# Re-ordering the start-up of an attention and mixture-of-experts kernel: query projections, heads and fills

## What is computed

```
q = heads(layernorm(x) @ Wq.T + bq)            # 16 heads of 16
k, v = heads(ctx @ Wk.T + bk), heads(ctx @ Wv.T + bv)
p = softmax(where(mask == 0, -1e9, q k^T / sqrt(16)))
x = x + (p v) @ Wo.T + bo                      # one batch after the other
f = layernorm(x)
w, e = top2(softmax(f @ router_w))             # 8 experts
x = x + sum over the two: w * (silu(f @ w1[e]) @ w2[e])
```

## Time and profile before

| | us |
|---|---|
| runs | 520.27, 520.72, 523.5 |
| median | 520.72 |
| the profiled execution's own time | 524.17 |
| its span (first to last instruction) | 522.4 |

### The profile page before, as it was taken

The page is one execution under the profiler, slowest core; times in us unless marked ns, Lnnn a source line. Parts: engine busy times, 40 slices in busy tenths (PEclk is TensorE's granted clock), DMA queues, the critical chain, the costliest instruction groups (busy, mean ns, idle before and its releaser), DMA issues.

```text
span 522.4 us, 10734 instructions
## 1 busy us (share of the span) xinstructions
PE 435.2 (83%) x4179; PEld 390.2 (75%) x4179; DVE 355.2 (68%) x756; ACT 256.0 (49%) x323; POOL 211.2 (40%) x170
## 2 busy tenths in 40 slices
PE   2567669999999999999999975477999999999700
PEld 2355458888888888888877874477999999999600
DVE  2776555777787777777776576944777777777425
ACT  3240244655665665656555533015566666666200
POOL 7270460223233333332100070052588887886410
PEclk9795787999999999999999988558999999999965
DMA  7849473777888887677430043072677777775148
GB/s 181 239 138 286 137 194 82 157 165 166 182 168 173 174 180 170 159 167 145 110 83 22 4 156 127 0 261 82 212 242 243 246 240 251 247 248 189 63 156 286
DMA packets 75026, 87.89 MB, mean 168 GB/s; under 512 B 20144, under 2 KB 66896, under 8 KB 74976
## 3 DMA queue, kind: packets, MB, share of 16 engines
q1 hardware_dynamic: 69040, 74.36, 54.8%
q0 software_dynamic: 4032, 11.02, 5.8%
q10 hardware_dynamic: 1904, 1.84, 1.0%
HBM read 51.58 MB, written 16.90 MB: 131 GB/s over the span
## 4 chain that ended last, share of the span: by engine, by line
PE 72%; DVE 11%; issue 7%; DMA 4%; POOL 2%; SPq 1%; ACT 1%; POOLq 0%; DVEq 0%; ACTq 0%
PE ps L1336 32%; PE ps L1396 11%; PE ps L1425 8%; PE ps L1411 8%; PE ps L1359 7%; DMA chosen_y<-y_rows 2%; PE ps L1644 2%; DVE neg_max L931 1%; SPq L527 1%; PE ps L1438 1%; PE ps L1627 1%; DVE x_rows_sb L978 1%; DVE w_lo L1232 1%; DMA keep<-keep_scratch 1%; PE ps L1446 1%
## 5 line engine op out<-in xcount | busy, mean ns | idle before, releaser
L931 DVE TENSOR_REDUCE neg_max<-ps 112x1 f32<-112x376 f32 x256 | 132.6, 546 | 45.0 <-PE ps L1396 41.2
L734 ACT ACTIVATE probs<-ps 125x1344 f32<-125x1344 f32 x64 | 82.8, 1293 | 57.6 <-PE ps L1411 56.7
L1396 PE MATMUL ps<-k_stack,q_stack 98*112 98x376 f32 x256 | 85.4, 376 | 11.0 <-issue 6.4
L555 POOL TENSOR_TENSOR k_lo<-k_f,k_hi 128x752 fp32r<-128x752 f32 x16 | 28.8, 1800 | 136.6 <-ACT k_hi L708 134.1
L679 POOL DMA_INDIRECT y_rows<-y_out,y_row_of_row x42 | 66.1, 1575 | 32.9 <-DVE y_out L1247 21.6
L1396 PEld LDWEIGHTS ps<-k_stack,q_stack 98*112 98x112 f32 x256 | 43.0, 181 | 25.1 <-DVE neg_max L931 14.3
L671 POOL DMA_INDIRECT rows<-xn_rows,token_of_row x42 | 42.1, 1003 | 48.5 <-DVE y_row_of_row L1191 32.2
L1411 PE MATMUL ps<-q_stack,k_stack 100*125 100x224 f32 x384 | 54.4, 278 | 1.2 <-ACT probs L734 0.9
L1336 PE MATMUL ps<-w_hi,h_hi 128*128 128x256 f32 x168 | 49.6, 295 | 5.6 <-issue 3.7
L1411 PEld LDWEIGHTS ps<-q_stack,k_stack 100*125 100x125 f32 x384 | 50.3, 191 | 2.3 <-ACT probs L734 1.7
L1336 PE MATMUL ps<-flat_t_hi,w_hi 128*128 128x256 f32 x168 | 48.9, 291 | 2.8 <-DVE flat_t_lo L1227 2.8
(11 more groups left out here) (191 smaller groups left out, 1005.9 us busy)
## 6 DMA issues: line engine op xcount, KB each, us to landing
w_raw<-w SPq DMA_DIRECT2D x42, 512.0 KB
k_stack<-k_hi SPq DMA_DIRECT2D x64, 188.0 KB, 4.7
k_stack<-k_lo SPq DMA_DIRECT2D x32, 188.0 KB, 5.5
ctx_raw<-ctx_t SPq DMA_DIRECT2D x32, 187.5 KB, 2.6
q_stack<-q_scratch SPq DMA_DIRECT2D x32, 168.0 KB
q_scratch<-q_hi SPq DMA_DIRECT2D x16, 224.0 KB, 3.1
xn_rows<-xn SPq DMA_DIRECT2D x14, 256.0 KB, 2.5
chosen_y<-y_rows SPq DMA_DIRECT2D x14, 256.0 KB, 5.4
```

Of the source, the lines that this page charges most:

```text
L555: pool.tensor_tensor(kl[:, :, :], kf[:, :, :], kh[:, :, :].bitcast(F32), ALU.subtract)\
L734: act.activation(pf[j % 2][:, :, :], ps[0:CT, BK_ST:BK_ST + KT, 0:4 * S], ACT.Exp).then_inc(pf_ready, 1)
L931: dve.tensor_reduce(neg_max[:, s:s + 1], ps[0:S, BK_MAX + s % 2, 0:CP], AX.X, ALU.max, negate=True).then_inc(max_read, 1)
L1396: pe.matmul(ps[0:S, BK_MAX + a, 0:CP], qs[b.ring][0:R_MAX, q, S * a:S * (a + 1)], ks[b.ring][0:R_MAX, q, :], start=True, stop=True).then_i ...
```

## The change

- The queries' weights are scaled by 1/4 as they are split (ACT `activation` with scale, DVE with multiply and subtract), and the bias once, so that a query leaves PSUM finished: ACT writes the high part straight from PSUM with the bias, and DVE the low part from PSUM, the bias and the high part. `q_f`, `queries` and POOL's `query_low` are gone. Both now work half by half, as do `x_high` and `x_low`.
- The rows of group 0 are normalised by DVE as before, those of groups 1 to 3 by ACT (x*rstd + nbias, four instructions; DVE makes the small `nbias`).
- Batch 0's `q_stack` is filled straight from `q_hi` and `q_lo` in SBUF (`stack_first_queries`, six transfers), not through the scratch; only from batch 1 on the scratch is read.
- `x` comes in as four loads, `keep` is made and written first, the queries' weights come before the biases, and the mask rows later. The output's weights and the router's move from the ramp's end into turn 1 on ACT and DVE.
- The low part of the first context goes from POOL to DVE, and POOL makes six fills at once after the mask rows. ACT takes a square root of a constant first, which loads its table there.
- PE has the heads of batch 0 in pairs among the query groups 1 to 3; the last half of group 3 comes after head 15 and `max_transpose`. SP writes `stack_max` of batch 0 before group 3's writes.

The core of the diff:

```diff
             def x_high(g):
-                act.wait_ge(xt_done, g + 1)
-                act.copy(xh[g % 2][:, :, :], ps[:, 0:2, 0:SG]).then_inc(xh_ready, 1)
+                for k in range(KD):
+                    act.wait_ge(xt_done, KD * g + k + 1)
...
+                    act.copy(xh[g % 2][:, k, :], ps[:, k, 0:SG]).then_inc(xh_ready, 1)
...
-                act.copy(qh[g % 2][:, :, :], qf[:, :, :]).then_inc(qh_ready, 1)
+                act.activation(qh[g % 2][:, t, :], ps[:, (2, BK_OUT)[t], 0:SG], ACT.Identity, bias=bq_c[:, t:t + 1])\
+                    .then_inc(qh_ready, 1)
...
+            def normalise_x(g):
+                act.wait_ge(nbias_ready, g)
+                for b in range(GB * g, GB * (g + 1)):
+                    last = act.activation(xr[:, b, :], xr[:, b, :], ACT.Identity, bias=nbias[0:S, b:b + 1],
+                                          scale=rstd[0:S, b:b + 1])
+                last.then_inc(xn_ready[g], 1)
...
+            def q_low(g):
 
                 for t in range(KD):
-                    dve.wait_ge(qproj_done, 2 * g + t + 1)
-                    if g and t == 0:
-                        dve.wait_ge(ql_ready, g)
-                    dve.tensor_scalar(qf[:, t, :], ps[:, (2, BK_OUT)[t], 0:SG], bq_c[:, t:t + 1], DK ** -0.5,
-                                      ALU.add, ALU.mult).then_inc(qf_ready, 1)
+                    dve.wait_ge(qh_ready, KD * g + t + 1)
+                    dve.scalar_tensor_tensor(out=ql[g % 2][:, t, :], in0=ps[:, (2, BK_OUT)[t], 0:SG],
+                                             scalar=bq_c[:, t:t + 1], in1=qh[g % 2][:, t, :].bitcast(F32),
+                                             op0=ALU.add, op1=ALU.subtract).then_inc(ql_ready, 1)
...
+            def stack_first_queries():
+
+                for a in range(KD):
+                    sp.wait_ge(qh_ready, a + 1)
+                    for c, src in enumerate((qh[0], qh[0], ql[0])):
+                        if c == 2:
+                            sp.wait_ge(ql_ready, a + 1)
+                        part = (0, 2, 1)[c]
+                        sp.dma_start(qs[0][2 * part + a:R_MASK:2 * PARTS, :, S * a:S * (a + 1)].bitcast(F32),
+                                     src[:, a, 0:S].bitcast(F32)).then_inc(q_stacked[0], 16)
...
             mask_rows()
-            ctx_low(first)
+            fill(range(0, 6))
+            key_low(first)
             pool.wait_ge(cl_ready, 1)
-            fill(range(0, 2))
-            key_low(first)
             ctx_low(second)
-            query_low(0)
-            pool.wait_ge(ql_ready, 1)
-            fill(range(2, 6))
             key_low(second)
-            query_low(1)
-            query_low(2)
             ctx_low(first.after(2))
-            query_low(3)
             for p in range(2):
                 pool.wait_ge(q_written[p], 96 * NG // 2)
...
+            ctx_low_first()
             x_stats(0)
-            normalise_x(0)
+            x_rstd(0)
+            normalise_first()
...
-            queries(0)
+            q_low(0)
             attn_weight_low(2)
+            x_stats(2)
             x_low(1)
-            x_stats(2)
-            normalise_x(2)
+            x_rstd(2)
             keys(second, 0)
             keys(second, 1)
-            queries(1)
+            maxima(first, range(0, 4))
+            q_low(1)
+            maxima(first, range(4, 6))
             x_low(2)
-            maxima(first, range(0, 8))
             x_stats(3)
-            normalise_x(3)
-            queries(2)
+            x_rstd(3)
+            maxima(first, range(6, 10))
+            q_low(2)
+            maxima(first, range(10, 14))
             x_low(3)
-            queries(3)
-            maxima(first, range(8, H))
+            maxima(first, range(14, H))
             max_rows(first)
+            q_low(3)
```

SP, at the start:

```diff
             sp.wait_ge(zeros_set, 1)
             load_ctx(first)
-            load_rows(slice(0, GB), xr_first_in)
+            load_rows(slice(0, GB), xr_in[0])
+            load_weight(1, wq_t)
+            sp.wait_ge(keep_ready, 1)
+            sp.dma_start(keep_scratch, keep_all[:, :]).then_inc(keep_written, 16)
...
+            sp.wait_ge(keep_written, 16)
+            load_keep(first)
+            load_rows(slice(GB, 2 * GB), xr_in[1])
...
-            load_rows(slice(GB, B), xr_rest_in)
-            sp.wait_ge(mask_written, 32)
-            load_keep(first)
```

More of the change, by code:

```diff
@@ L186, in xattn_moe_kernel @@
         x2 = sb("x2", [P, NT, D])
-        assert cursor["at"] <= queries_end, "x2 lies where the queries were"
+        queries_end = max(queries_end, cursor["at"])
         cursor["at"] = raw_at
@@ L438, in write_queries @@
                                      src[g % 2][:, t, :].bitcast(F32)).then_inc(q_written[g % 2], 16)
-            second = first.after(1)
+            second, third = first.after(1), first.after(2)
             sp.dma_start(m_all[:, 0:C], mask).then_inc(mask_in, 16)
@@ L779, in _, with late_weights @@
             key_high(second)
-            q_high(1)
+            normalise_x(2)
+            queries_high(1)
             x_high(2)
             x_std(3)
-            q_high(2)
+            normalise_x(3)
+            queries_high(2)
+            ctx_high(third)
             x_high(3)
-            ctx_high(first.after(2))
-            q_high(3)
-            key_high(first.after(2))
-            attn_weight(3)
-            act.wait_ge(rw_in, 16)
-            act.copy(rwh[:, :, :], rw_raw[:, :, :]).then_inc(rw_ready, 1)
+            queries_high(3)
+            key_high(third)
+            def late_weights():
+                attn_weight(3)
+                act.wait_ge(rw_in, 16)
+                act.copy(rwh[:, :, :], rw_raw[:, :, :]).then_inc(rw_ready, 1)
             def turn(b):
@@ new lines, in normalise_first @@
+            def normalise_first():
+                for b in range(GB):
+                    last = dve.tensor_scalar(xr[:, b, :], xr[:, b, :], moments[0:S, b, 0:1], rstd[0:S, b:b + 1],
+                                             ALU.subtract, ALU.mult)
+                last.then_inc(xn_ready[0], 1)
+            def x_low(g):
+                for k in range(KD):
+                    dve.wait_ge(xh_ready, KD * g + k + 1)
+                    dve.tensor_tensor(xl[g % 2][:, k, :], ps[:, k, 0:SG], xh[g % 2][:, k, :].bitcast(F32),
+                                      ALU.subtract).then_inc(xl_ready, 1)
@@ L1518, in x_transpose, with project_queries, keys @@
                                             ident[0:S, 0:S])
-                last.then_inc(xt_done, 1)
-            def project_queries(g):
-                pe.wait_ge(wl_ready, 2)
-                pe.wait_ge(xl_ready, g + 1)
-                for t in range(KD):
-                    if g >= 1:
-                        pe.wait_ge(qf_ready, 2 * g - 1 + t)
-                    m = slice(t * P, (t + 1) * P)
-                    product(ps[:, (2, BK_OUT)[t], 0:SG],
-                            [(w[:, 1, k, m], x[g % 2][:, k, :]) for k in range(KD)
-                             for w, x in ((wh, xh), (wl, xh), (wh, xl))]).then_inc(qproj_done, 1)
+                    last.then_inc(xt_done, 1)
+            def project_queries(g, t):
+                if g == 0 and t == 0:
+                    pe.wait_ge(wl_ready, 2)
+                if g:
+                    pe.wait_ge(ql_ready, KD * (g - 1) + t + 1)
+                m = slice(t * P, (t + 1) * P)
+                terms = [(w, x, k) for k in range(KD) for w, x in ((wh, xh), (wl, xh), (wh, xl))]
+                for n, (w, x, k) in enumerate(terms):
+                    if x is xl or n % 3 == 0:
+                        pe.wait_ge((xh_ready, xl_ready)[x is xl], KD * g + k + 1)
+                    last = pe.matmul(ps[:, (2, BK_OUT)[t], 0:SG], w[:, 1, k, m], x[g % 2][:, k, :],
+                                     start=n == 0, stop=n == len(terms) - 1)
+                last.then_inc(qproj_done, 1)
+            def keys(b):
+                for t in range(KD):
+                    for k in range(KD):
+                        project_keys(b, t, k)
+            second, third = first.after(1), first.after(2)
             pe.wait_ge(wl_ready, 1)
-            for t in range(KD):
-                for k in range(KD):
-                    project_keys(first, t, k)
+            keys(first)
             x_transpose(0)
-            project_queries(0)
+            project_queries(0, 0)
+            project_queries(0, 1)
             x_transpose(1)
@@ L1541, in _ @@
                 project_values(first, k3)
-            for t in range(KD):
-                for k in range(KD):
-                    project_keys(first.after(1), t, k)
-            project_queries(1)
-            x_transpose(2)
-            pe.wait_ge(filled, 6)
-            head_scores(first, range(0, 8))
-            project_queries(2)
+            keys(second)
+            pe.wait_ge(filled, 6)
+            head_scores(first, range(0, 2))
+            project_queries(1, 0)
```

(21 more changed lines are left out.)

160 lines of the change are left out of this document (94 added, 66 removed).

## The result

| | before | after |
|---|---|---|
| median, 20 runs each | 520.24 us | 517.73 us |
| ratio, 95% interval | | 0.995 (0.9928 to 0.9972) |
| profiled execution, span | 524.17, 522.4 | 518.43, 516.6 |

The change gains half a per cent, 2.6 us by the ratio (1.5 to 3.7), where 5.7 us were forecast. The time itself, 517.7 us where 515.0 was forecast, is inside the stated range, but the gain is less than half of the forecast's. One slow run of the kernel before, 710.42 us, is left out of the ratio.

A forecast was written before the change was run, and what follows sets the result against it. The chain from the last q_lo through POOL's ctx_lo to PE's restart was taken as the bound. The ramp's -6.05 us and +0.3 in turn 1 gave -5.75, so 520.72 - 5.7 = 515.0 us, range 512.5 to 517.5.

The forecast's parts named there:

- What bounds the kernel: Ramp into turn 0: PE restarts 14.85 us after the last q_lo, released by POOL's ctx_lo of batch 3.
- First part: Ramp until the first head: starts at 32.2 us (30.2 or 34.1 by the clock) instead of 41.57, gain 9.4.
- rival 3: Ramp: values' w_lo held by POOL's ctx_lo, 1.3 us lost, last group late behind heads; 522.9 us, chance 0.10.
- second meeting: Ramp: the first context's low part on DVE held beside POOL's mask rows, costing up to 1.2 us.
- Second part: Ramp from first head to last q_lo: 21.5 us at high clock, 27.3 at low, 24.4 taken.
- The ramp's sum: Last q_lo at 57.5 us instead of 63.55, PE's restart at 72.4: gain 6.05 us.
- What moves into turn 1: Output's and router's weight splitting behind turn 1: 0 if slack swallows it, 0.9 if not, 0.3 us taken.
- The forecast's own range: Whole kernel's time: 512.5 to 517.5 us, by a third of the way to either clock.
- 1: Ramp rival: fills do no harm, clock stays high, SP becomes the bound; gain 9.4, 511.3 us, chance 0.20.
- 2: Ramp rival: low clock all along, last q_lo at 62.3, gain 1.25; 519.8 us, chance 0.25 together with 4.
- 4: Turn 0 rival: the gate moves but PE is late, gain less than 6 us; chance included in 2's 0.25.
- Turns of equal length afterwards: Sign that the forecast is right: after the ramp, the attention turns all last equally long.

The follow-up runs named there:

- e11: The changed kernel run again unchanged: 517.60 us, ratio 0.9948 to the kernel before.
- e8: Changed kernel, late weights back in the ramp, POOL's k_lo and ctx_lo ahead of the last group's wait, SP stacking keys before queries in turn 0: 512.91 us.
- e4: Changed kernel with four of POOL's six early fills put behind the first group's normalisation: 516.69 us, ratio 0.9919 to the kernel before.
- e7: Changed kernel, late weights back in the ramp, POOL's ctx_lo of batch 1 waiting for the values' w_lo: 512.34 us.
- e1: Changed kernel with the output's and router's weights split at the ramp's end again, not after turn 1: 514.00 us, ratio 0.9889 to the kernel before.
- e6: Changed kernel, late weights back in the ramp, second half of query group 3 ahead of heads 14 and 15 and the transposed maxima: 512.71 us.
- e12: Same kernel as e1, run again beside e11: 515.56 us, ratio 0.9895 to the kernel before.
- e15: The kernel before, unchanged, run once more for another profile of its ramp: 520.31 us.
- e5: Changed kernel with DVE's share of the late weights after turn 2, ACT's left after turn 1: 515.02 us, ratio 0.9925 to the kernel before.

## Why the prediction was wrong

**What bounds the kernel**: right. From the last `q_lo` to PE's restart 14.85 us was forecast, 14.26 measured (14.3 to 14.5 in the eight other profiles of the new start that keep this gate). POOL's `ctx_lo` ended just ahead of the restart each time.

**First part**: too short. The first head was to come at 32.2 (30.2 or 34.1 by the clock). It came at 35.94 in the profile, at 33.38 in e11, and at 33.5 to 34.2 in six others with the same start; only e8 had 35.9 again. The terms: the normalisation ended at 16.06, the forecast's limit, not at 15.0. `keep`, which was to be there by 12, was hidden behind that; if e4's wait ahead of `k_f` is for it, it came only at 14.9. ACT's four rows took 2.07 us, not 1.44, so the copy from PSUM was no measure for this `activation`. `q_hi`'s half took 0.62, not 0.54. And the values' `w_lo` took 1.91 us, not 0.69, and ended at 27.23 instead of 25.2. From there to the first head the forecast had 5.0 us at the high clock and 8.9 at the low one, and this held: 5.15 in e7, 8.7 in the shown profile and e8, between them elsewhere.

The long `w_lo` was rival 3's mechanism, and it is real (e7). The Trainium skill, page "SBUF — State Buffer", section "Who interferes with whom", states it: a DVE instruction with two SBUF inputs contends with a GpSimd instruction that reads SBUF. Three instructions of e7 and e8 agree. It made the instruction 1.2 us longer, about the 1.3 that rival 3 gave it. But rival 3's second meeting did not come (DVE's first `ctx_lo` took 0.94 us in every profile of the new start), and its second part at the low clock, 28.2 us, did not either.

**Second part**: 24.4 us forecast, 22.9 in the profile, in e1 and in e11. In most profiles it was too long by about as much as the first was too short, so that the last `q_lo` (57.5 forecast) ended at 56.3 to 57.1; in the shown one it ended at 58.86. That the two errors met so well is luck. That the last half group pays for standing behind the heads holds (e6, 1.6 us).

**The ramp's sum**: 6.05 us forecast. The restart moved by 5.3 us in the two profiles. With the late weights back in the ramp the gain is 4.9 us by the medians (520.1 less 515.2), and 5.8 and 5.5 by the ratios of e1 and e12, so 6.05 is not excluded. What the steps left out is that the end moves with the last `q_lo` only if the clock behind the gate is the same. The changed kernel stands there for 7.5 to 8 us (5.0 in e1 and e12, where the late weights hold DVE for 2.1 us ahead of it), and in all six profiles it has the low clock after it. The old one stood 3 us with the low clock after it in three profiles of four, but not in e15. From the restart to turn 0's transposed maxima it took 8.1 to 9.3 us in those nine profiles and 6.46 in e15. How often each happens is not measured.

**What moves into turn 1: the step that failed.** It was priced at 0.3 us, at most 0.9, as work that DVE's and ACT's slack swallows. It costs 2.5 us by undoing it and 3.7 by doing it alone. The work is worth what was said, 0.3 us (e5). Left out was the wait that the move makes: what DVE's `w_lo` waits for, what is queued behind it, and that PE has no more than two banks of slack. Where the clock falls behind the stop of 1.2 us, as in two profiles of five, it doubles the loss.

**The forecast's own range** was 512.5 to 517.5, "by a third of the way to either clock". A third of the 4.9 us to either clock is 1.6, so it should have been 513.4 to 516.6; 2.5 is half of the way. The first head at the low clock adds up to 34.0, not 34.1. Neither slip changes the failed step.

**Rivals.** Neither 1 nor 2 happened as told: the fills did harm and the clock changed between its levels. Nor did 4: POOL's `ctx_lo` let PE go on. "Turns of equal length afterwards" was named as the sign of being right, and a loss beyond turn 1 as what would make the forecast wrong; this it was.

## What to carry to other kernels

Work that is moved out of a stretch where everyone waits into one where an engine is full must be priced by its waits, not only by its length. Put each engine's share behind a point where its input is long ready, and look at what is queued behind it. When a gate is opened, look for the next thing that hangs on the same event, and move that with it; alone, such an edit may show only a part of its worth. And before a gain is read from a pair of profiles, see how far each lies from its own median.

## What the runs showed of the hardware

- A stop of 1.20 us in a PE that was full is followed by the half clock in two of the five profiles that have it (the shown one and e11), and the turn then costs 3.0 us more than the others instead of 1.5.
- The same start gave a first head at 33.4 to 34.2 us in seven profiles and at 35.9 in two. The granted clock goes with it: 0.50 from 30 to 36 us in the shown one, 1.00 in e11, with PE busy for 5.45 of these 6 us in both. What sets it is open.
- POOL's memsets held four DVE `tensor_scalar` for 5.05 us (1.38 without them, in e4). DVE's `w_lo` of the queries, with two SBUF inputs, ran beside a memset in e4 at its usual 0.68, but the values' `w_lo` beside POOL's subtraction at 1.91. A `router_lo` of 0.17 us was held for 1.73 (e8).
